# A decoder layer in which the start of the first self-attention is reordered: weights loaded in three parts, batch 0's keys roped on VectorE, its first stacks issued from two queues

## The reference

```python
x = _layernorm(x + attn(x, Wqkv, Wout))            # rope on q and k, softmax(q k^T / 4) v
x = _layernorm(x + xattn(x, ctx, w_q, b_q, ...))   # same shape, no rope, with biases
x = _layernorm(x + ffn(x, gate_w, we_gate, ...))   # top-2 of 8 experts + shared experts
...
# rope, per head:
q = q * cos + rotate_half(q) * sin
k = k * cos + rotate_half(k) * sin
```

## Time and profile before

| | |
|---|---|
| median of 3 runs | 1466.65 us (1461.20 to 1470.51) |
| profiled execution | 1462.47 us |
| its span, first to last instruction | 1460.7 us |
| mean granted TensorE clock | 0.954 |
| busy share: PE, DVE, ACT, POOL | 91%, 74%, 63%, 32% |
| first product of two matrices | 16.8 us |
| first row maxima scores | 41.9 us |
| first scores of `own0` | 63.8 us |

### The profile page before, as it was taken

How to read it: one execution, slowest core, us unless ns; L and a number is a source line. 1 busy time by engine, 2 the same in 40 slices (tenths; PEclk the granted TensorE clock), 3 DMA queues, 4 the chain that set the end, 5 groups by cost and what they waited for, 6 DMA issues and landing times. The chain is left out here.

```text
span 1460.7 us, 27397 instructions
## 1 busy us (share of the span) xinstructions
PE 1336.0 (91%) x8424; PEld 810.1 (55%) x8424; DVE 1083.1 (74%) x2218; ACT 924.3 (63%) x1766; POOL 464.6 (32%) x485
## 2 busy tenths in 40 slices
PE   2799999999999999999999999998588999999974
PEld 2434444444444445444444444434577889999964
DVE  4688789888978978987998888892476445555475
ACT  3177777777677776777777777774354445655543
POOL 5234203302501510330240201101155436666753
PEclk9599999999999999999999999997698799999997
DMA  3553444344334424424434442210345337786752
GB/s 123 126 187 113 132 131 134 107 133 132 118 115 130 137 73 145 136 83 141 119 117 124 139 135 75 88 45 16 124 168 181 105 118 133 131 168 135 149 181 82
DMA packets 108090, 179.91 MB, mean 123 GB/s; under 512 B 20288, under 2 KB 65984, under 8 KB 103872
## 3 DMA queue, kind: packets, MB, share of 16 engines
q1 hardware_dynamic: 93376, 159.11, 35.2%
q0 software_dynamic: 14592, 19.41, 7.5%
HBM read 98.09 MB, written 79.30 MB: 121 GB/s over the span
## 5 line engine op out<-in xcount | busy, mean ns | idle before, releaser
L746 DVE TENSOR_REDUCE nm<-ps_ring 128x1 f32<-128x512 f32 x1024 | 638.6, 680 | 57.9 <-PE ps_ring L919 57.2
L705 ACT ACTIVATE prob<-ps_sc 128x512 f32<-128x512 f32 x1024 | 551.4, 600 | 197.5 <-PE ps_sc L934 196.7
L919 PE MATMUL ps_ring<-qk 48*128 48x512 f32 x1024 | 405.2, 467 | 18.8 <-DMA qk<-hbm_self 12.8
L934 PE MATMUL ps_sc<-qk 50*128 50x512 f32 x1024 | 390.1, 454 | 11.3 <-ACT prob L705 10.3
L934 PEld LDWEIGHTS ps_sc<-qk 50*128 50x128 f32 x1024 | 162.0, 187 | 303.3 <-ACT prob L705 219.2
L951 PE MATMUL ps_out<-prob,va 128*32 128x512 f32 x2048 | 276.7, 613 | 2.3 <-ACT prob L705 1.2
L1695 PE MATMUL ps_gu<-x2f,we 128*128 128x256 f32 (+1 forms) x1344 | 220.1, 318 | 4.9 <-DVE h L1586 2.5
L1695 PEld LDWEIGHTS ps_gu<-x2f,we 128*128 128x128 f32 x1344 | 187.8, 190 | 21.7 <-DVE h L1586 3.4
L919 PEld LDWEIGHTS ps_ring<-qk 48*128 48x128 f32 x1024 | 166.3, 188 | 49.1 <-DVE nm L746 27.6
L1695 PE MATMUL ps_dn<-we,hf 128*128 128x256 f32 x864 | 124.0, 300 | 12.8 <-DVE totals L1669 10.9
L544 POOL TENSOR_TENSOR rstd<-mv,eps 128x2 f32<-128x2 f32 x32 | 6.3, 197 | 377.2 <-DVE mv L815 377.2
(11 more groups left out here) (154 smaller groups left out, 1612.0 us busy)
## 6 DMA issues: line engine op xcount, KB each, us to landing
qk<-hbm_self SPq DMA_DIRECT2D x384, 64.0 KB, 2.4
qk<-hbm_cross SPq DMA_DIRECT2D x384, 64.0 KB, 2.4
hbm_self<-stage SPq DMA_DIRECT2D x16, 1024.0 KB, 3.9
hbm_cross<-stage SPq DMA_DIRECT2D x16, 1024.0 KB, 3.9
slots_x<-zeros SPq DMA_DIRECT2D x8, 1360.0 KB, 5.9
xs<-slots_x SPq DMA_DIRECT2D x40, 272.0 KB
weraw<-w_moe SPq DMA_DIRECT2D x11, 768.0 KB
x2in<-x SPq DMA_DIRECT2D x16, 512.0 KB, 4.6
```

What stands on the lines that cost most here:

```text
L705: nc.scalar.activation(prob[:, s % 2, j, :], ps_sc[:, score_bank(h.cur, HG * s + j), :], ACT.Exp, scale=HD ** -0.5).then_inc(exp_done[a], 1)
L746: nc.vector.tensor_reduce(nm[:, g % 2, r:r + 1], bank(slot), axis=AX.X, op=ALU.max, negate=True).then_inc(max_done[a], 1)
L919: nc.tensor.matmul(bank(slot), qk[rows, 0, pair, P * c:P * c + P], qk[rows, 1, pair, :], start=True, stop=True).then_inc(smax_done[a], 1)
L934: nc.tensor.matmul(ps_sc[:, score_bank(inst, n), :], qk[rows, 1, h // 2, P * c:P * c + P], qk[rows, 0, h // 2, :], start=True, stop=True). ...
```

## The change

The first loads are cut differently. The weights come in three parts: `QK` (columns of queries and keys of self-attention, 512 of each half), `VO` (its values and output projection, 512) and `REST` (those of cross-attention, 1024). `QK` is loaded first, then batch 0's input, the tables, `VO`, the small tables and `REST`. `QK` and `VO` are staged in `prob` as before, `REST` in the room of `x1b` and `x1c`, which now lie in one tensor, `residual`. ScalarE and VectorE split `QK` first and then the input (its low part moves from GpSimd to VectorE); `VO` is split inside `own`, and `REST` in `own0` (high part by ScalarE in step 6, low part by GpSimd in step 7). The fills of `va` move to GpSimd. For batch 0 the keys' sine product, sum and low part are done by VectorE, the queries' stay on GpSimd. Of stacks 0 and 1 of batch 0 the parity-1 half (six DMAs each) is issued from ScalarE's queue (`share_of_stack`), in steps 4 and 7 of `own`.

```diff
-            for a in (SELF, CROSS):
-                sp.dma_start(staged_w(a), w_att[:, :, columns(a)]).then_inc(raw_w[a], 16)
+            sp.dma_start(staged_self[:, :, QK], w_att[:, :, QK]).then_inc(raw_w[0], 16)
+            sp.dma_start(raw[:, :, :], xT[0, :, :, :]).then_inc(in_sem["x"], 16)
             sp.dma_start(trig[:, :, :], tables).then_inc(consts_dma, 16)
+            sp.dma_start(staged_self[:, :, VO], w_att[:, :, VO]).then_inc(raw_w[1], 16)
             sp.dma_start(bcol[:, :, :], b_cols).then_inc(consts_dma, 16)
             sp.dma_start(bo[:, :], bo_rows).then_inc(consts_dma, 16)
+            sp.dma_start(staged_rest, w_att[:, :, REST]).then_inc(raw_w[1], 16)
...
+                        if on_vector("k", b):
+                            sp.wait_ge(lo_done["q"], upto("q", b, m))
                         sp.dma_start(hbm_self[m], stage[:, m, :, :].bitcast(F32)).then_inc(self_out[m], 16)
...
+                    if h.name == "own0" and s == 7:
+
+                        pool.wait_ge(w_hi, 4)
+                        nc.gpsimd.tensor_tensor(w[:, LO, :, REST], staged_rest, w[:, HI, :, REST].bitcast(F32),
+                                                ALU.subtract).then_inc(consts, 1)
                     for kind, n, b in h.table.get(s, []):
+                        if on_vector(kind, b):
+                            continue
...
+            def weights_hi(of, staged):
+
+                act.wait_ge(raw_w[1], 32)
+                nc.scalar.activation(w[:, HI, :, of], staged, ACT.Copy).then_inc(w_hi, 1)
+
+            def share_of_stack(g):
+
+                act.wait_ge(self_out[0], 16)
+                rows = slice(64 * g, 64 * g + 64)
+                for r, (qp, kp) in enumerate(((HI, HI), (HI, LO), (LO, HI))):
+                    for s, part in ((0, qp), (1, kp)):
+                        row = SIDE + HD * r
+                        act.dma_start(qk[row:row + HD, s, 2 * g:2 * g + 2, :].bitcast(F32),
+                                      hbm_self[0, rows, 2 * s + part, :].rearrange("(h y d) t -> y d h t", y=2, d=HD)[1]) \
+                            .then_inc(stack_in[SELF][g], 16)
...
+                    if h.name == "second" and isinstance(h.k, int) and h.k == -1:
+                        if s == 2:
+                            weights_hi(VO, staged_self[:, :, VO])
+                            act.wait_ge(consts_dma, 48)
+                        if s == 4:
+                            act.wait_ge(consts, 6)
+                            act.wait_ge(w_ready, 1)
+                            share_of_stack(0)
+                        if s == 7:
+                            share_of_stack(1)
+                    if h.name == "own0" and s == 6:
+                        weights_hi(REST, staged_rest)
...
+                    if on_vector(kind, b):
+                        dve.wait_ge(read[kind], upto(kind, b, n))
+                        nc.vector.tensor_tensor(rot[:, c, :], rot[:, c, :], trig[:, 1, :], ALU.mult).then_inc(sin_done[kind], 1)
+                        dve.wait_ge(sin_done[kind], upto(kind, b, n))
+                        nc.vector.tensor_tensor(cosq[:, c, :], cosq[:, c, :], rot[:, c, :], ALU.add).then_inc(roped[kind], 1)
...
+                    if kind == "v" and isinstance(b, int) and b == 0:
+                        pe.wait_ge(w_ready, 3)
...
                 if h.name == "own0":
-                    pe.wait_ge(w_ready, 5)
-                if h.name == "own1":
-                    pe.wait_ge(consts, 7)
+                    pe.wait_ge(consts, 10)
+                if h.name == "own2":
+                    pe.wait_ge(consts, 11)
```

More of the change, by code:

```diff
@@ L237, in before_loop @@
     lead = first(-1)
[L238 removed]
+    lead.loads, lead.clear = {}, None
     own = second(-1, lead)
@@ L319, in attention_phase @@
         x1 = sb("x1", [P, TT, D])
-        x1b = sb("x1b", [P, TT, D])
-        x1c = sb("x1c", [P, TT, D])
+        residual = sb("residual", [P, 2, TT, D])
+        x1b, x1c = (residual[:, n, :, :] for n in range(2))
         st6 = sb("st6", [P, TT, 6])
@@ L376, in wait_done, with shared_stack, on_vector @@
                 eng.wait_ge(s, upto(kind, b, n))
+        def shared_stack(inst, g):
+            return isinstance(inst[1], int) and inst == (SELF, 0) and g < 2
+        def on_vector(kind, b):
+            return isinstance(b, int) and b == 0 and kind in ("x", "k", "kf")
         def place_of(n):
@@ L410, in stack @@
                 a, b = inst
+                parities = (0,) if shared_stack(inst, g) else (0, 1)
                 m, rows = g // 2, slice(64 * (g % 2), 64 * (g % 2) + 64)
@@ L421, in stack @@
                         src = (hbm_cross if a else hbm_self)[m, rows, 2 * s + part, :]
-                        for par in range(2):
+                        for par in parities:
                             row = SIDE * par + HD * r
@@ L510, in _ @@
             pool.wait_ge(consts, 6)
-            nc.gpsimd.memset(va[:, 2, :, :, HD:2 * HD], 1.0).then_inc(consts, 1)
             nc.gpsimd.memset(mone[:, :, :], -1.0).then_inc(consts, 1)
-            pool.wait_ge(consts, 8)
+            for room in range(3):
+                nc.gpsimd.memset(va[:, room, :, :, HD:2 * HD], 1.0).then_inc(consts, 1)
+            pool.wait_ge(consts, 10)
             pool.wait_ge(consts_dma, 48)
@@ L575, in _ @@
                                  ACT.Copy).then_inc(w_hi, 1)
-            for a in (SELF, CROSS):
-                act.wait_ge(raw_w[a], 16)
-                nc.scalar.activation(w[:, HI, :, columns(a)], staged_w(a), ACT.Copy).then_inc(w_hi, 1)
-            act.wait_ge(consts_dma, 48)
+            act.wait_ge(raw_w[0], 16)
+            nc.scalar.activation(w[:, HI, :, QK], staged_self[:, :, QK], ACT.Copy).then_inc(w_hi, 1)
+            def weights_hi(of, staged):
[10 more added lines that the diff above has]
+                            .then_inc(stack_in[SELF][g], 16)
             def split_hi(kind, b, n, out, value, bias=None):
@@ L820, in half @@
                     turn = h.maxima(s)
+                    if h.name == "second" and isinstance(h.k, int) and h.k == -1:
+                        if s == 0:
+                            dve.wait_ge(consts_dma, 48)
+                        if s == 4:
+                            weights_lo(VO, 3)
                     for kind, n, b, of in h.behind(s):
```

27 lines of the change are left out of this document (16 added, 11 removed).

## The result

| | before | changed |
|---|---|---|
| median | 1464.39 us (6 runs, 1460.19 to 1470.51) | 1455.15 us (6 runs, 1453.20 to 1457.53) |
| ratio, 95% interval | | 0.9935 [0.9907, 0.9963] |
| span of the profiled execution | 1460.7 us | 1455.8 us |
| first product | 16.80 us | 9.88 us |
| first row maxima scores | 41.93 us | 33.53 us |

The forecast was 1457, 0.65% less than before. The measurement gives 0.65% (0.37 to 0.93). On two later occasions, each with the kernel before on the same chip, the changed kernel gave 0.9950 [0.9937, 0.9963] and 0.9961 [0.9943, 0.9978]. The mean of the three is 0.9949, which is 7.5 us of 1464.

The account below looks back on a forecast made before the run. TensorE's two idle stretches, together 29.6 us, were taken to bound the kernel. Terms 7.15 + 1.6 + 1.85 + 0.3 - 1.4 = 9.5 us gave 1457.1 us against 1466.65, range 1449 to 1464.

Parts of the forecast that it names:

- First product: TensorE's first idle stretch: smaller loads and new splits bring the first product from 16.80 to about 9.65 us, gain 7.15.
- Key block 0: Batch 0's first key block: three instructions on VectorE gain another 1.6 us, with its write issued at 21.9.
- Stack 0: Twelve stack DMAs before the first row maxima: two queues take 5.6 us instead of 7.45, gain 1.85.
- The second queue brings nothing: Rival on the stack DMAs: DMA engines limit or ScalarE issues are dear; 1.85 us or more lost, chance 0.12.
- Row maxima: From first maxima to `own0`: same instructions as before, less a VectorE idle of 0.28 us, counted as 0.3 gained.
- `REST` in `own0`: Step 6 of `own0`: ScalarE's high part of `REST` puts 1.4 us on the path, bounds 0 and 1.9.
- The sum: Whole kernel: the terms add to a gain of 9.5 us, forecast 1457.1 us, 0.65% less.
- the clock comes back sooner: Rival from the maxima into `own0`: cutting TensorE's pause restores the clock, gain 14.5 us in all, or 1452; chance 0.22.
- Slower through a low `own0`: Rival in `own0`: the clock stays low throughout, 19 us lost, ending at 1476; chance 0.04.
- wrong if the span behind `own0`'s start changes by more than 3 us: Sign in the profile behind `own0`'s start: lengths should stay unchanged, and over 3 us difference refutes the prediction.

Follow-up runs that it names:

- e9: The changed kernel, unedited, run again on a third chip; ratio 0.9961 [0.9943, 0.9978] to the kernel before.
- e4: Changed kernel with batch 0's keys roped and split by GpSimd again; ratio 0.9972 [0.9955, 0.9989] to the kernel before.
- e7: Changed kernel plus 14 extra TensorE products ahead of value job 0 and 22 behind it; ratio 0.9983 [0.9963, 1.0004] to the kernel before.
- e11: The kernel of e2 again, on a third chip: changed kernel with stack 1 issued by SyncE alone; ratio 0.9938 [0.9915, 0.9962] to the kernel before.
- e3: Changed kernel with both parts of `REST` split in step 9 of `own` instead of in `own0`; ratio 0.9936 [0.9916, 0.9957] to the kernel before.
- e8: The kernel before, unedited, run as a control on a third chip; ratio 1.0010 [0.9994, 1.0026] to the kernel before.
- e2: Changed kernel with stack 0 on two queues but stack 1 issued by SyncE alone; ratio 0.9925 [0.9911, 0.9939] to the kernel before.
- e1: Changed kernel with all twelve DMAs of stacks 0 and 1 issued by SyncE again; ratio 0.9944 [0.9926, 0.9962] to the kernel before.
- e5: Changed kernel with the edits of e1 and e4 together: one queue, keys on GpSimd; ratio 0.9969 [0.9953, 0.9986] to the kernel before.
- e6: Changed kernel with the edits of e2 and e3 together; ratio 0.9955 [0.9936, 0.9973] to the kernel before.
- e10: The kernel of e6 again, on a third chip; ratio 0.9960 [0.9945, 0.9975] to the kernel before.

## Why the prediction was right, step by step

**First product.** Forecast 9.65, measured 9.88, 9.99 and 10.49 in three profiles of the changed kernel: a gain of 6.9 in the first, instead of 7.15. Right. VectorE's two splits took 1.23 each rather than 1.12. In e9 `QK` was there 0.4 us later (ScalarE starts on it at 6.48, not 6.07).

**Key block 0.** Forecast 1.6 more, write at 21.9; measured 21.98, 1.7 more. Right, with the hold-up, and e4 prices it alone at 2.1. One condition was left out: I took the first key job at the lower level (2.97 us until VectorE reads it), as it ran in the changed kernel's first profile. In e7, e9 and e11 it ran at the upper one, VectorE read it 1.7 us behind its start, and the write came 11.5 us behind the first product instead of 12.1. Of the 1.3 us gained half went again, since VectorE's addition now met GpSimd's low part of the query (e9):

```profile
18.42 1.39 POOL L530 TENSOR_TENSOR stage<-cosq,stage 128x512 fp32r<-128x512 f32 x1 [0.74 <-ACT stage L618]
18.71 1.66 DVE L815 TENSOR_TENSOR cosq<-cosq,res 128x512 f32<-128x512 f32 x1
```

The kernel before has no such gain: its write comes 13.8 us behind the first product in both profiles, though the job ran at the lower level in one and the upper in the other; there GpSimd's chain sets the time. The Trainium skill's rule on the shared port (SBUF — State Buffer, "Who interferes with whom") agrees with the trace: 0.98 for 0.69 on VectorE, and in e4 2.20 for 1.23.

**Stack 0.** This step failed. I had put 1.85 us between an issue bound of 4.7 and a transfer bound of 6.5; measured is 7.69, 7.67 and 7.25 in three profiles of the changed kernel, which is no gain. The step that failed is the middle of the two, 5.6 us; two things were missed in it. The first is in size: two queues press 183 GB/s through full DMA engines, near the 173 of the earlier trace rows, so the transfer bound of 6.5 was the least that was seen and not one end: of ten stacks on two queues none took under 6.65. The second is a mechanism, and likely rather than shown: I followed ScalarE's second batch of issues only as far as its other work, and not into the DMA engines, where it runs among the packets of stack 0. Where it is taken away the stack takes 6.96 on average, else 7.35. "The second queue brings nothing" was my rival with a chance of 0.12, and it is the case that came true. The total stayed inside because that rival was only 1.85 us away. The Trainium skill's sentence that a second issuing engine saves only the time of initiating (DMA: Bandwidth & Descriptors, "Issuing engines are not separate DMA queues") would have given the gain of 8.7 to this point; 8.4 was measured. I set it aside because issuing was 5.45 of 7.45, and the trace sided with the sentence and not with me.

**Row maxima.** I counted 0.3 for a wait for stack 1 as gone; it is still 0.28. I had misread: the row names no stack, and TensorE's pause of 1.30 us there ends with VectorE's reductions, before and after alike. From the first maxima to `own0` passed 21.81 us, before 21.86.

**`REST` in `own0`.** Forecast 1.4 with 0 to 1.9 as bounds; e3 measures 0.84, and the lead fell by 0.84 over these steps. What I left out is the other thing that can end them, the row of maxima behind the stack on SyncE's queue.

**The sum.** With measured terms it is 6.9 + 1.7 - 0.2 - 0.8 = 7.6 us, against 9.5 forecast. The mean of the three measured ratios is 7.5 us; that the first, 9.2, matched my number so closely was luck.

**The rivals.** That the clock comes back sooner because the pause is cut was wrong as a cause. Over the row maxima it averages 0.50 to 0.60 in all fourteen profiles, in e7 filled pauses didn't keep it up, and e8 and e9 show that its early or late return in `own0` goes with neither kernel. Slower through a low `own0` wasn't seen; the longest return was 6.5 us in. My test "wrong if the span behind `own0`'s start changes by more than 3 us" was badly chosen: it changed by 3.6 us (1396.9 before, 1400.5 after) and of the change only the 0.84 us of `REST` is in it. The lead grew from 8.45 us at `own0`'s start to 9.1 at the last evacuation but one of the attention phase, and it was 7.5 when the first weights of the experts were asked for (1031.3 us before, 1023.8 changed). Part of that loss goes with the clock: from the last evacuation to that request it stood at the lower level for 18.0 us, in the kernel before for 13.9. The last 2.6 us go inside the experts, whose instructions the change doesn't touch, and what took them stays open. That such differences come and go shows in the other pair. Between 100 and 980 us the equivalent of 3.4 us and of 20.5 us passed at the lower level in e8 and e9, and when the experts' weights were asked for nothing was left of the 8.8 us that `own0` had come earlier (1029.34 in e8, 1029.39 in e9). The 2.9 us by which the profiled spans of that pair differ came back inside the experts. So one pair of profiles can't show that a head start arrives; the medians of 6 to 29 runs do, 7.2 to 9.2 us on each occasion.

## What to carry to other kernels

When a chain of small DMAs looks bound by its issuing, work out the other bound first, from a stretch in which the DMA engines are full: if the two lie close, a second queue buys little, and what that queue issues next may delay the transfer that is waited for. A head start at the front of a long in-order kernel does arrive at the end, but price what the moved work costs at its new place, by what else ends the same stretch. For differences below half a per cent, compare marks inside several profiles (start of a phase, distance between two evacuations) to see what a part of the change does at its place, and the medians of many runs to see that it arrives; one pair of profiled spans here would have shown 4.9 us, another 2.9, for a gain of 7.5.

## What the runs showed of the hardware

- DMAs of 64 KB in 2 KB rows, issued from two queues, filled the DMA engines (share 0.99 in the changed kernel, 0.96 in e2) at 183 and 184 GB/s; from one queue the share was 0.60 at 134 GB/s (e1).
- Of a VectorE and a GpSimd instruction that both read two inputs in SBUF and overlap, the one that started later was the longer one. VectorE later: 0.98 us for 0.69 (changed), 2.20 for 1.23 (e4), 1.66 for 0.69 (e9). GpSimd later: 2.31 for 1.26 (e5). A difference of 0.2 us in their starts decided in e4 and e5 which engine paid 1 us.
- SyncE's twelve issues of one stack took 5.4 to 5.9 us in some places and 6.2 to 8.5 in others, and at one place of one kernel 5.75 in one profile and 7.07 in the next (before and e8). In e6, where they took 7.37, TensorE waited 1.3 us for what stands behind them.
- The granted clock averaged 0.58 over the changed kernel's row maxima, a stretch of 21.81 us in which TensorE was busy for 19.68 (0.50 to 0.60 over the fourteen profiles); in e7 it fell to 1.2 GHz 0.7 us into them, behind 5.28 us of dense products at 2.4 GHz and 2.1 us of rest.
- The first six products took 2.90 us in every kernel, the rate of the lower level (six of the same form take 1.66 at the upper and 2.89 at the lower level later in the changed kernel), while the profile's granted clock reads 1.00 in that stretch.
- The clock differs between executions of one kernel: the profiles of two equal kernels (e6 and e10) differed by 17 us in the time spent at the lower level between 100 and 980 us (23.8 and 6.8).
